# Reading each spread of expert gates as four transfers of 32 rows from four stored copies

## What is computed

```python
gate_v = _get_sel_gate(x, sel_v_w, rs)        # [B, S, H, E], two of eight chosen
gate_o = _get_sel_gate(x, sel_o_w, rs)
xv = jnp.einsum('bsd,hedp->bshep', x, v_w.reshape(H, E, D, P))
v = jnp.einsum('bshep,bshe->bhsp', xv, gate_v)
att = jax.nn.softmax(jnp.einsum('bhqp,bhkp->bhqk', q, k) * SCALE, axis=-1)
ctx = jnp.einsum('bhqk,bhkp->bqhp', att, v)
weighted = ctx[:, :, :, None, :] * gate_o[..., None]
out = jnp.einsum('bshep,hepd->bsd', weighted, o_w.reshape(H, E, P, D))
```

## Time and profile before

| what | value |
|---|---|
| median of 3 runs | 785.13 us (782.28 to 785.24) |
| the profiled execution, its own time | 786.33 us |
| its span | 785.0 us |
| TensorE, VectorE, ScalarE, GpSimd busy | 88%, 63%, 48%, 23% |
| moved by the DMA engines | 113.72 MB, of it 64 MB spreads (128 x 512 KB) and 32 MB weight tiles (64 x 512 KB) |
| mean granted TensorE clock | 0.93 of full speed |

### The profile page before, as it was taken

How to read it: one execution, slowest core, us unless ns; L and a number is a source line. 1 busy time by engine, 2 the same in 40 slices (tenths; PEclk the granted TensorE clock), 3 DMA queues, 4 the chain that set the end, 5 groups by cost and what they waited for, 6 DMA issues and landing times.

```text
span 785.0 us, 14588 instructions
## 1 busy us (share of the span) xinstructions
PE 688.7 (88%) x5496; PEld 604.3 (77%) x5496; DVE 496.0 (63%) x1289; ACT 373.4 (48%) x1281; POOL 181.6 (23%) x256
## 2 busy tenths in 40 slices
PE   5768987889999998889999989699899997879887
PEld 4568886557899998587899978597899994557766
DVE  1756455847847758765676767694857857254535
ACT  2510102773351665635345576546465634646483
POOL 1000004433011131415300150335201506420040
PEclk9869999899999999889999999889999998798969
DMA  9669895007946730087475410274425700000000
GB/s 359 256 174 324 307 316 185 1 8 234 305 165 223 264 119 1 26 250 261 161 228 182 161 56 2 63 269 167 166 95 176 267 4 7 1 1 1 1 1 8
DMA packets 33190, 113.72 MB, mean 145 GB/s; under 512 B 3680, under 2 KB 7264, under 8 KB 32736
## 3 DMA queue, kind: packets, MB, share of 16 engines
q1 hardware_dynamic: 33120, 112.78, 42.3%
HBM read 111.72 MB, written 1.05 MB: 144 GB/s over the span
## 4 chain that ended last, share of the span: by engine, by line
PE 43%; DVE 25%; DMA 15%; ACT 6%; POOL 5%; issue 4%; SPq 0%; POOLq 0%; DVEq 0%
PE bank L460 24%; DMA spread<-gates_of 15%; PE f_bank L460 14%; DVE gated L1432 7%; ACT wide_b L1104 3%; PE bank L656 2%; DVE wide_b L1435 2%; POOL rstd L1323 2%; DVE x L1435 2%; PE f_bank L553 1%; DVE f_route L1432 1%; DVE max_neg L1693 1%; POOL wide_b L1332 1%; DVE f_max_neg L1511 1%; ACT f_b L1040 1%
## 5 line engine op out<-in xcount | busy, mean ns | idle before, releaser
L460 PE MATMUL f_bank<-weights,gated 128*128 128x128 f32 x2048 | 253.9, 282 | 22.8 <-DVE gated L1432 22.5
L460 PEld LDWEIGHTS f_bank<-weights,gated 128*128 128x128 f32 x2048 | 242.3, 196 | 32.2 <-issue 21.7
L1104 ACT ACTIVATE wide_b<-wide_b,max_neg 128x120 f32<-128x120 f32 x272 | 103.5, 384 | 48.1 <-DVE max_neg L1693 42.7
L1432 DVE TENSOR_TENSOR gated<-spread,f_b 128x1024 f32<-128x1024 f32 x64 | 79.5, 1258 | 44.1 <-DMA spread<-gates_of 20.4
L1432 DVE TENSOR_TENSOR gated<-spread,f_xnT 128x1024 f32<-128x1024 f32 x64 | 80.9, 1269 | 37.1 <-DMA spread<-gates_of 34.6
L1332 POOL TENSOR_TENSOR wide_b<-wide_b,row_inv 128x480 f32<-128x480 f32 x64 | 71.6, 1122 | 127.3 <-DVE row_inv L1698 127.3
L1323 POOL TENSOR_TENSOR rstd<-var_eps,w_const 128x1 f32<-128x1 f32 (+1 forms) x56 | 38.2, 683 | 251.3 <-DVE var_eps L1428 251.2
L989 ACT ACTIVATE wide_a<-bank 120x512 f32<-120x512 f32 (+4 forms) x109 | 57.6, 544 | 62.2 <-PE bank L460 23.6
L656 PE MATMUL bank<-w_const,wide_b 128*120 128x128 f32 x256 | 46.5, 319 | 11.8 <-POOL wide_b L1332 11.7
L1104 ACT ACTIVATION_READ_ACCUMULATOR wide_b<-wide_b,max_neg 128x1 f32 x272 | 51.6, 190 | 0.0
L656 PEld LDWEIGHTS bank<-w_const,wide_b 128*120 128x120 f32 x256 | 33.4, 159 | 22.9 <-issue 21.2
(11 more groups left out here) (236 smaller groups left out, 1179.0 us busy)
## 6 DMA issues: line engine op xcount, KB each, us to landing
spread<-gates_of SPq DMA_DIRECT2D x128, 512.0 KB, 5.5
weights<-in_experts SPq DMA_DIRECT2D x64, 512.0 KB, 6.4
w_L2f<-in_L2f SPq DMA_DIRECT2D x1, 2124.0 KB, 15.2
w_L3x<-in_L3x SPq DMA_DIRECT2D x1, 2108.0 KB, 19.2
wide_b<-in_raw0f SPq DMA_DIRECT2D x1, 1024.0 KB, 6.2
w_L3f<-in_L3f SPq DMA_DIRECT2D x1, 1000.0 KB, 20.5
w_L1f<-in_L1f SPq DMA_DIRECT2D x1, 516.0 KB, 9.8
x_next<-in_x SPq DMA_DIRECT2D x4, 128.0 KB, 5.0
```

The costliest lines, as they stand in the source:

```text
L460: return nc.tensor.matmul(o, lhsT, rhs, start=first, stop=last)
L1104: last = nc.scalar.activation(p, p, ACT.Exp, bias=max_neg[lane][:, h:h + 1], accum_out=row_sum[lane][:, h:h + 1])
L1432: return nc.vector.tensor_tensor(o, a, c, op)
```

## The change

`gates_of` gets a leading dimension of 4 copies, 128 KB apart. The store of each transposed half writes all four copies in one transfer, whose source is read four times (256 KB instead of 64 KB). Each spread becomes four transfers of 32 rows: rows 0 to 31 from copy 0, rows 32 to 63 from copy 1, and so on, issued one behind the other by SP, each adding 16 to the same semaphore. VectorE waits for four times as much. The four copies hold the same values, so all of the arithmetic is the same.

```diff
-W_SLOTS, G_SLOTS = 4, 3
+W_SLOTS, G_SLOTS, COPIES = 4, 3, 4
...
                     if n >= G_SLOTS:
                         sp.wait_ge(f_gated_ready, n - G_SLOTS + 1)
-                    sp.dma_start(spread[n % G_SLOTS][:, :],
-                                 gates_of[row:row + E, :].rearrange("e s -> (e s)").partition_broadcast(128))\
-                        .then_inc(f_spread_loaded[n % G_SLOTS], 16)
+                    for c in range(COPIES):
+                        sp.dma_start(spread[n % G_SLOTS][32 * c:32 * c + 32, :],
+                                     gates_of[c, row:row + E, :].rearrange("e s -> (e s)").partition_broadcast(32))\
+                            .then_inc(f_spread_loaded[n % G_SLOTS], 16)
...
                         sp.wait_ge(f_gateT_ready[t], pair + 1)
-                        sp.dma_start(gates_of[128 * t:128 * t + 128, :], f_gateT[t][:, :]).then_inc(f_gates_stored[t], 16)
+                        sp.dma_start(gates_of[:, 128 * t:128 * t + 128, :].rearrange("c g s -> g c s"),
+                                     f_gateT[t][:, :].unsqueeze(1).broadcast_to([128, COPIES, S])).then_inc(f_gates_stored[t], 16)
...
                         slot = n % G_SLOTS
-                        dve.wait_ge(f_spread_loaded[slot], 16 * (n // G_SLOTS + 1))
+                        dve.wait_ge(f_spread_loaded[slot], 16 * COPIES * (n // G_SLOTS + 1))
...
-    gates_of = nc.dram_tensor("gates_of", (256, S), F32, kind="Internal").ap()
+    gates_of = nc.dram_tensor("gates_of", (COPIES, 256, S), F32, kind="Internal").ap()
```

## The result

The changed kernel takes 824.46 us (median, 816.04 to 828.72) where the kernel before takes 785.09 us in the same series: ratio 1.0475, 95% interval 1.0392 to 1.0557: 39 us slower by the medians, 37 us by the ratio. The ratio leaves out the run of 828.72 us, a slow one (over 1.5% above the fastest). The span of the profiled execution is 822.7 us against 785.0.

What follows compares the result with a forecast made beforehand. Spreads into SBUF were taken as the bound, in pair 0 through the DMA engines. 20 pieces x (0.96 + 0.45) = 28 us plus 3 us of stores: 786.3 + 31 - 1.2 = 816 us, range 768 to 845 us.

Steps and rivals of the forecast that it cites:

- half-rate rival: Writing of spreads: every quarter at half rate, 2.64 us per spread, 51 us more, 835 us; chance 0.28.
- What bounds the kernel: Spreads into SBUF in four stretches: 20 chain pieces of 6 us; in pair 0 the DMA engines bind.
- Writing 32 rows at a time: Quarters' writes into SBUF: 1.98 us per spread against 1.83, so 0.45 us per loop of three spreads.
- SP's issues: SP's queue: three more issues per spread make the last quarter later, 0.96 us per piece of the chain.
- Reading from four copies: Spreads' reads in device memory: copies could save up to 0.5 us per spread, but most of that gain is excluded.
- The faster rival: Spreads' packets in the dense stretches: crowded reading goes, 1.32 us per spread, 772 us; chance 0.25.
- The store of four copies: Eight gates stores grow from 64 KB to 256 KB: 0.7 us per pair, in sum 3 us.
- The page's price of 840 us: Spreads at the skill page's 189 GB/s: 2.8 us each, a loop 2.8 us longer, the kernel ending at about 840 us.
- The objection that quarters may mix and keep both halves busy: Against half rate: quarters of different spreads may mix as DMA engines drift apart, so both halves are busy at once.
- the chain's share of spreads: Spreads' share of the whole chain, 15% before: above 18% if the forecast is right, under 13% if crowding goes.
- the rate near 265 GB/s: GB/s at full DMA share in the first spreads after 44 us: 265 as forecast, 350 or more if relieved.
- One sign I had named as fatal: Spread pieces of the chain: if they keep 6 us, the forecast is wrong at its root.

Runs made afterwards that it cites:

- e3: Against the kernel before: each spread is two transfers of 64 neighbouring rows from one copy; 825.1 us, ratio 1.0469.
- e6: Against the kernel before: each spread is two transfers from one copy, one writing the even rows, one the odd; 784.82 us, ratio 0.9886.
- e12: Against the kernel before: two transfers per spread, even and odd rows, from one copy, run again with more rounds; 784.41 us, ratio 0.9998.
- e7: Against the kernel before: SP issues three tiny transfers into an unread scratch tile ahead of each whole spread; 808.34 us, ratio 1.0215.
- e1: Against the changed kernel: four quarters of 32 rows still, but all read one copy and the store is 64 KB; 820.02 us, ratio 1.0397 to the kernel before.
- e4: Against the kernel before: four copies stored, each spread one transfer of 128 rows with neighbouring rows reading different copies; 788.49 us, ratio 0.9994.
- e8: Against the kernel before: each spread reads 128 different rows of expert weights instead of one gates row, so the output differs; 774.39 us, ratio 0.9777.
- e10: Against the changed kernel: the quarters are issued in the order 0, 2, 1, 3; 805.79 us, ratio 1.0255 to the kernel before.
- e5: Against the changed kernel: quarter c writes rows c, c+4, c+8 and so on instead of 32 neighbouring ones; 814.41 us, ratio 1.0277 to the kernel before.
- e2: Against the changed kernel: each of the four transfers is 128 rows by 256 columns instead of 32 rows by 1024; 827.88 us, ratio 1.0497 to the kernel before.
- e9: Against the kernel before: sixteen copies stored, each spread one transfer of 128 rows with eight neighbouring rows per copy; 830.79 us, ratio 1.0574.

## Why the prediction was right, and where it was off

The direction and the range held: 816 us was forecast, 824.5 us measured, between the forecast and its half-rate rival (835 us as written; its own terms give 786.3 + 51 - 1.2 = 836). The steps:

- *What bounds the kernel.* Right. All the loss is in the four stretches; outside of them nothing moved (48.6 us before the first tile, 147.8 after the last). Pair 0 runs at 97.8 / 31 = 3.15 us per tile where it ran at 2.45, and a loop of three tiles by measured rates is 3 x 2.31 + 1.5 x 1.32 = 8.9 us of DMA work for 9.5 us of time.
- *Writing 32 rows at a time.* This term was undersized. I took the middle of two bounds, 1.98 us per spread, for lack of a row; it measured 2.31 us in the first spreads, three quarters of the way to the doubling at 2.64, and 2.6 us from 60 to 80 us if the weight tiles there keep their rate, which is the doubling. Against 1.83 us, 2.31 is 0.48 us per spread where 0.15 stood in the sum. It is also the step that e3 and e6 prove by themselves: at the same issues the rows' places alone are worth 1.0469 against 0.9886, and against 0.9998 when e6 was repeated as e12.
- *SP's issues.* Adding this term to the rate term in full was not right. e3 keeps SP 2 x 0.60 us per spread, the change 4 x 0.42 us, the kernel before 0.32 us, and e3 loses as much as the change (1.0469 and 1.0475). The placement alone (e3, 4.7%) and the issues alone (e7, 2.2%) would add up to 6.8%, and the change lost 4.75%. So once the queue of transfers is full, a later issue mostly hides under it; how the loss of the change itself divides was not measured. That e7's 17.7 us is close to 20 x 0.96 = 19 us is luck: the lag was 1.4 us, not 0.96, because four issues stand 0.47 us apart, and it cost about two thirds of itself. The sum of 31 us came near 39 because one term was too small and the other was counted in full, which partly cancelled.
- *Reading from four copies.* Right to give it little: e1, without copies, is as slow as the change within the noise, and e4, with them in a whole transfer, is as fast as the kernel before. The faster rival is refuted, and e8 puts what the reading of one place costs at some 2%.
- *The store of four copies.* Its landing time moved as said (1.5 to 2.2 us). Its price of 3 us is 0.4%, which these runs can't tell from nothing: the ratio of e4, with those stores, is 0.9958 to 1.0030. The first tile starts at 48.6 us before and after. In e4 it comes 5.7 us after the copy of the second half of the gates where the kernel before takes 4.9 us and the changed one 5.1, which would fit 0.7 us per pair with most of it made up by first quarters that move sooner; that last part is not shown.
- *Half rate.* In pair 0 this rival came nearer than my forecast. A loop there grew by 21.8 / 31 x 3 = 2.1 us, where I had 1.4 and the rival 2.4. In the other three pairs my sum has 10 pieces x 1.41 = 14 us, the rival's 24, and 16 were measured. So the total lay between the two because the later pairs lost less than the rival's price and only pair 0 came close to it; nothing in the sum treated them differently, and that it held so well is partly luck. The page's price of 840 us, which the prediction calls left out, lies inside its range of 768 to 845 us. The objection that quarters may mix and keep both halves busy is in part supported by e10: order alone gives 260 instead of 227 GB/s. That quarters of different spreads mix by drift was not seen.

Of the signs named in advance: the chain's share of spreads was to be above 18%, or above 20% at half rate (18.3%); the rate near 265 GB/s in my case and 200 at half rate (227); VectorE's waits in pair 0 about 50 us (56.8); and pair 0 longer by some 14 us (21.8), for which the rival had 26 (106 for 80). They show the right mechanism and a rate term that was too small, with the rate and the length of pair 0 on the rival's side of the middle.

One sign I had named as fatal came, by its letter: the pieces of the chain kept 6 us. They are 25 now instead of 20, and 151 / 25 is 6.0 us. The sign was badly made. A piece now begins with the issue of the last quarter, and the issues before it stand in the chain as SP's own queue, 51 us that were 2 us before. Both together are 8.1 us per piece where they were 6.1. This sum separates nothing either, since the first quarters move while the later ones are issued; e3 against e6 does.

The Trainium skill's page (SBUF — State Buffer, "Door 1: The DMA port swizzle") is borne out in kind. Its ratio of 189 to 328 GB/s is 0.58. Here 227 GB/s is 0.57 of the 396 of the weight tiles at the start, but those read other places; held against spreads from the same place, e3's 229 and 250 GB/s are 0.75 and 0.73 of e6's 306 and 343 in the same windows, and 0.63 and 0.72 of e12's. Halves of 64 neighbouring rows were hardly faster than quarters of 32 (229 against 225 GB/s in e1), as it says. By its absolute figure the kernel would have ended at about 840 us; the measurement decides for 824.5. Its sentence that transfers on the two halves serialize ("Can I just issue two DMAs to hit both halves?") holds only in part here: in the order 0, 2, 1, 3 they gained 8 to 15% in rate.

## What to carry to other kernels

Splitting a transfer by rows is not free even when bytes, engines and queue stay the same: ask which rows one piece covers, and if a transfer must be split, let each piece span all 128 rows and count what each issue costs the queue that issues it: of the versions here whose pieces span them, two halves lost nothing, four strided quarters 2.8% and four column quarters 5.0%. Before curing a crowded source, measure its ceiling with a version that reads different places: here it was 2%, about what three more issues cost alone and under half of what the neighbouring rows cost. Where two limits lie on the same loop, don't add them unseen: here the loss was that of the larger (4.7 and 2.2% alone, 4.75% together).

## What was not expected

- The time that SP needs for one issue depends on the pattern: 0.32 us for 128 rows from one place, 0.42 us (median) for 32 neighbouring rows, 0.59 us for 32 strided rows and 0.60 us for 64 rows of either layout. In e5 this made SP the limit. A median can hide it: the column quarters of e2 have 0.43 us over the whole kernel and 0.60 us on average in pair 0.
- Swapping the two middle ones of four transfers brought 2.2% (a ratio of 1.0255 in place of 1.0475), without changing what any of them does.
- A whole transfer of 128 rows can run at 230 GB/s (e9), when its source pattern is 16 x 8 rows; the cause was only argued.
